# Six small edits in a two-layer conditioned mixture-of-experts kernel: warming products, first bias, lane tables, one row turn, shares

## What is computed

```
x = x + _L0_ffn_ref(_L0_cond_ref(x, cond_8, weight, mask, bias), router_w, expert_weights)
x = x + _L1_ffn_ref(_L1_cond_ref(x, cond_8, W_base, b_base, As, Bs), gate_w, exp_gate, exp_up, exp_down, sh_gate, sh_up, sh_down)
```

```
topk_vals, topk_idx = top_k(softmax(x @ router_w.T), 2)
topk_w = topk_vals / (topk_vals.sum(-1) + 1e-06)
out = ((combined + remap_bias) * weights).sum(axis=0)      # remap_bias = probs of the two
```

## Time and profile before

| | |
|---|---|
| runs, median of 3 | 354.28 us (354.05 to 354.62) |
| the profiled execution, its own time | 354.84 us |
| its span, first to last instruction | 353.1 us |
| granted TensorE clock, mean | 1.000 |
| busy: PE, PE weight load | 346.8 us (98%), 216.9 us (61%) |
| busy: DVE, ACT, POOL | 239.1 us (68%), 172.5 us (49%), 147.8 us (42%) |
| DMA | 47.42 MB, 134 GB/s over the span |

### The profile page before, as it was taken

How to read it: one execution, slowest core, us unless ns; L and a number is a source line. 1 busy time by engine, 2 the same in 40 slices (tenths; PEclk the granted TensorE clock), 3 DMA queues, 4 the chain that set the end, 5 groups by cost and what they waited for, 6 DMA issues and landing times.

```text
span 353.1 us, 8015 instructions
## 1 busy us (share of the span) xinstructions
PE 346.8 (98%) x2746; PEld 216.9 (61%) x2747; DVE 239.1 (68%) x618; ACT 172.5 (49%) x296; POOL 147.8 (42%) x252
## 2 busy tenths in 40 slices
PE   8999999999999999999999999999999999999996
PEld 4444444454455454566458777777777777766655
DVE  1369899997766754789985555555555565655696
ACT  1178468558558648544541333333333333424493
POOL 4049475656646644000012355555555555422000
PEclk9999999999999999999999999999999999999999
DMA  7976122442343321010005334444454353111963
GB/s 275 407 305 218 59 100 81 159 159 91 129 156 85 136 80 61 0 61 0 2 1 187 113 132 162 174 146 156 138 177 163 132 156 119 61 46 49 351 226 119
DMA packets 20505, 47.42 MB, mean 134 GB/s; under 512 B 2432, under 2 KB 11392, under 8 KB 20480
## 3 DMA queue, kind: packets, MB, share of 16 engines
q1 hardware_dynamic: 17024, 37.65, 29.9%
q0 software_dynamic: 3456, 9.44, 8.4%
HBM read 29.25 MB, written 8.91 MB: 108 GB/s over the span
## 4 chain that ended last, share of the span: by engine, by line
PE 81%; DVE 13%; ACT 3%; issue 3%; DVEq 0%; ACTq 0%
PE bank L1156 58%; PE bank L1167 7%; PE bank L1330 4%; PE bank L1433 4%; PE bank L1408 2%; DVE x L863 2%; PE bank L1182 2%; DVE prod L1045 2%; DVE yg L959 1%; ACT w1s L658 1%; ACT sil L669 1%; DVE acts L1053 1%; PE bank L1172 1%; PE bank L1246 1%; PE bank L1257 1%
## 5 line engine op out<-in xcount | busy, mean ns | idle before, releaser
L1156 PE MATMUL bank<-w0s,hs 128*128 128x512 f16 x384 | 86.5, 379 | 0.9 <-DVE x L863 0.9
L513 POOL TENSOR_TENSOR w1s<-piece,w1s 128x170 f16<-128x170 f32 x128 | 60.9, 514 | 42.4 <-ACT piece L600 42.4
L522 POOL DMA_INDIRECT rows<-token_store,row_in x36 | 35.0, 971 | 77.7 <-DVE row_in L990 45.3
L863 DVE SCALAR_TENSOR_TENSOR x<-bank,coef,x 128x256 f32<-128x256 f32 x128 | 54.4, 476 | 14.2 <-PE bank L1156 14.1
L1156 PEld LDWEIGHTS bank<-w0s,hs 128*128 128x128 f16 x384 | 37.1, 98 | 42.9 <-DVE x L863 1.4
L1156 PE MATMUL bank<-hs,w1s 128*128 128x512 f16 x264 | 59.4, 379 | 0.3 <-DVE prod L1045 0.2
L1156 PE MATMUL bank<-w1s,rT 128*128 x336 | 54.5, 313 | 0.0
L528 POOL DMA_INDIRECT results<-yb,row_out x36 | 35.7, 992 | 35.9 <-ACT yb L707 35.9
L701 ACT ACTIVATE ract<-prod 128x352 f16<-128x352 f32 x36 | 17.9, 497 | 53.9 <-DVE prod L1128 44.0
L1156 PEld LDWEIGHTS bank<-hs,w1s 128*128 128x128 f16 x264 | 25.3, 98 | 29.2 <-DVE prod L1045 1.3
L1156 PEld LDWEIGHTS bank<-w1s,rT 128*128 128x128 f16 x336 | 31.7, 98 | 14.7 <-issue 0.2
(11 more groups left out here) (183 smaller groups left out, 498.4 us busy)
## 6 DMA issues: line engine op xcount, KB each, us to landing
piece<-w SPq DMA_DIRECT2D x16, 680.0 KB, 4.0
xrow<-w1s SPq DMA_DIRECT2D x8, 704.0 KB, 3.6
xrow<-w1s SPq DMA_DIRECT2D x8, 384.0 KB, 3.0
w1s<-results SPq DMA_DIRECT2D x6, 512.0 KB, 10.0
x<-wc SPq DMA_DIRECT2D x4, 512.0 KB, 5.0
w1s<-xT SPq DMA_DIRECT2D x4, 512.0 KB, 9.7
w1s<-w SPq DMA_DIRECT2D x4, 512.0 KB, 9.1
x<-x SPq DMA_DIRECT2D x4, 512.0 KB, 8.4
```

The costliest lines, as they stand in the source:

```text
L513: ins = nc.gpsimd.tensor_tensor(w1s[:, LO, at], piece[:, i % 2, part], w1s[:, HI, at], ALU.subtract)
L522: pool.indirect_dma_start(rows[:, i % 2], None, token_store, bass.IndirectOffsetOnAxis(row_in[:, slot_tile(i):slot_tile(i) + 1], 0)).then_ ...
L863: nc.vector.scalar_tensor_tensor(x1[:, t], bank[(n + a) % 4][:, h * D:(h + 1) * D], coef[:, t, e:e + 1], x1[:, t], ALU.mult, ALU.add).then ...
L1156: mm = nc.tensor.matmul(out_ap, l, r, start=(i == 0), stop=(i == len(terms) - 1))
```

## The change

Six edits:

1. `FILL` goes from 14 to 4.
2. In `shares0` the sum over `ex` is issued first and isn't linked, and the scaling of `REC` is merged into the instruction that makes `coef`. The four instructions of the bias become `bias0`, called after m = 0, j = 1 for part 0, and directly after `shares0` for the other parts.
3. ACT's `exps(0)` comes after `w0_scaled(1)`.
4. The last 12 of 32 lane instructions go to POOL, behind its last piece and a new semaphore `s_slots` that `slots(1)` sets; `inverse()` waits for them by `s_lanes`. DVE issues 20, in `accumulate(0)`. The entries of `between` for i = 8, 9 and 10 move up by one.
5. The rows of tile 2 are turned in step -1 (before tile 1's gate product) and not in step 0.
6. `shares1` is called in `accumulate(1)`, one part after each of its four adds, and the written-out steps at the end of DVE's loop become three.

```diff
@@ -77,7 +77,7 @@
     WARM = 8
-    FILL = 14
+    FILL = 4
     DIRECT = (0, 2)
@@ -264,6 +264,8 @@
             "s_hot",
+            "s_slots",
+            "s_lanes",
             "s_inv",
@@ -366,7 +368,7 @@
 
-        def run_tiles(eng, step, ahead, beside=None):
+        def run_tiles(eng, step, ahead):
 
@@ -376,8 +378,6 @@
                 step(s, s % 2)
-                if beside is not None:
-                    beside(s)
 
@@ -513,6 +513,12 @@
 
+            pool.wait_ge(sm["s_pclo"], NP)
+            pool.wait_ge(sm["s_slots"], 1)
+            for n in range(5 * ENTRIES // 8, ENTRIES):
+                ins = nc.gpsimd.tensor_scalar(hot_lo[:, n], lane16[:], slot_lo[:, n:n + 1], None, ALU.is_equal)
+            ins.then_inc(sm["s_lanes"], 1)
+
             pool.wait_ge(sm["s_tok"], 16 * B)
@@ -569,8 +575,8 @@
             w0_hi(1)
+            w0_scaled(1)
             exps(0, PARTS[0], 1.0 / (SH0 * SW))
-            w0_scaled(1)
             h_hi(0, 2)
@@ -791,14 +797,17 @@
                 dve.wait_ge(sm["s_exp"], part + 1)
+                nc.vector.tensor_reduce(SUM[:, tiles], ex[:, tiles], AX.X, ALU.add)
                 link(nc.vector.tensor_tensor(t1[:, tiles], ex[:, tiles], t1[:, tiles], ALU.mult))
                 link(nc.vector.tensor_reduce(S2[:, tiles], t1[:, tiles], AX.X, ALU.add))
-                link(nc.vector.tensor_reduce(SUM[:, tiles], ex[:, tiles], AX.X, ALU.add))
                 link(nc.vector.scalar_tensor_tensor(S2[:, tiles], SUM[:, tiles], EPS_TOPK, S2[:, tiles], ALU.mult,
...
                 link(nc.vector.reciprocal(REC[:, tiles], S2[:, tiles]))
-                link(nc.vector.tensor_scalar(REC[:, tiles], REC[:, tiles], 1.0 / (SH0 * SW), None, ALU.mult))
-                link(nc.vector.tensor_tensor(coef[:, tiles], t1[:, tiles], each(REC, tiles), ALU.mult))
+                link(nc.vector.scalar_tensor_tensor(coef[:, tiles], t1[:, tiles], 1.0 / (SH0 * SW), each(REC, tiles),
+                                                    ALU.mult, ALU.mult))
+
+            def bias0(tiles):
+
                 link(nc.vector.tensor_tensor(t1[:, tiles], t1[:, tiles], coef[:, tiles], ALU.mult))
@@ -865,6 +874,8 @@
                         h_lo(0, 3)
+                    if m == 0 and j == 1:
+                        bias0(PARTS[0])
                     if m == 0 and j == 2:
@@ -873,6 +884,7 @@
                         shares0((m + 1) // 2, PARTS[(m + 1) // 2])
+                        bias0(PARTS[(m + 1) // 2])
                     if j == 0 and m >= 3 and m % 2 == 1:
@@ -890,21 +902,21 @@
 
-            def shares1(s):
-
-                if s == TILES - 5:
+            def shares1(q):
+
+                if q == 0:
                     dve.wait_ge(sm["s_exp"], 4)
...
                     link(nc.vector.tensor_reduce(S2, t1[:], AX.X, ALU.add))
-                if s == TILES - 4:
+                if q == 1:
                     link(nc.vector.reciprocal(REC, S2))
...
                     link(nc.vector.tensor_tensor(coef[:], t1[:], each(REC, ALL), ALU.mult))
-                if s == TILES - 3:
+                if q == 2:
                     link(nc.vector.tensor_tensor(t1[:], oh1[:], coef[:], ALU.mult))
                     link(nc.vector.tensor_reduce(W1, t1[:], AX.X, ALU.add))
-                if s == TILES - 2:
+                if q == 3:
                     link(nc.vector.tensor_tensor(t1[:], oh2[:], coef[:], ALU.mult))
@@ -949,8 +961,10 @@
                     link(nc.vector.tensor_copy(slot_hi[:], idx[:].rearrange("p k t -> p (k t)")))
-                    link(nc.vector.scalar_tensor_tensor(slot_lo[:], slot_hi[:], -float(P),
-                                                        st[:, 7:9].rearrange("p k t -> p (k t)"), ALU.mult, ALU.add))
+                    nc.vector.scalar_tensor_tensor(slot_lo[:], slot_hi[:], -float(P),
+                                                   st[:, 7:9].rearrange("p k t -> p (k t)"), ALU.mult,
+                                                   ALU.add).then_inc(sm["s_slots"], 1)
+                    dve.wait_ge(sm["s_slots"], 1)
 
@@ -1066,15 +1080,18 @@
                     t = c * TPB + q
-                    if c == 0:
+                    if c == 0 and q < 2:
                         hot_lanes(2 * q)
-                        if q < TPB - 1:
-                            hot_lanes(2 * q + 1)
+                        hot_lanes(2 * q + 1)
+                    if c == 0 and q == 2:
+                        hot_lanes(2 * q)
                     if c == 1 and q == TPB - 2:
...
                                                    ALU.mult, ALU.add).then_inc(sm["s_acc"], 1)
+                    if c == 1:
+                        shares1(q)
                     if c == 2 and q == 1:
@@ -1086,8 +1103,8 @@
 
-            between = {2: lambda: take_logits(1, 0, ALL), 3: chosen, 5: groups, 6: lambda: slots(0), 7: lambda: hot_tiles(0, 0), 8: lambda: hot_lanes(7),
-                       9: lambda: hot_tiles(0, 1), 10: lambda: hot_tiles(1), 11: lambda: hot_tiles(2, 0),
+            between = {2: lambda: take_logits(1, 0, ALL), 3: chosen, 5: groups, 6: lambda: slots(0), 7: lambda: hot_tiles(0, 0),
+                       8: lambda: hot_tiles(0, 1), 9: lambda: hot_tiles(1), 11: lambda: hot_tiles(2, 0),
                        12: lambda: hot_tiles(2, 1), 13: lambda: tile_experts(0), 14: lambda: tile_experts(1),
@@ -1133,7 +1150,7 @@
             dve.wait_ge(sm["s_ahi"], EARLY)
-            run_tiles(dve, step, 4, shares1)
+            run_tiles(dve, step, 2)
             step(TILES, TILES % 2)
@@ -1366,6 +1383,7 @@
                 pe.wait_ge(sm["s_hot"], 2)
+                pe.wait_ge(sm["s_lanes"], 1)
                 pe.wait_ge(sm["s_acc"], TPB)
@@ -1397,16 +1415,22 @@
 
+            def turn_rows(i, par):
+
+                pe.wait_ge(s_row[par], landed(i, par))
+                for a in range(2):
+                    for k in range(KT):
+                        o = (a * KT + k) * P
+                        mm = nc.tensor.transpose(bank16[4][:, o:o + P], rows[:, par, o:o + P], ident16[:])
+                mm.then_inc(sm["s_ra"], 1)
+
             def step(s, par, down_at, gate_at, down_own=None, gate_own=None):
...
                 i = s + 2
-                if known(i) and again(i):
-                    pe.wait_ge(s_row[par], landed(i, par))
-                    for a in range(2):
-                        for k in range(KT):
-                            o = (a * KT + k) * P
-                            mm = nc.tensor.transpose(bank16[4][:, o:o + P], rows[:, par, o:o + P], ident16[:])
-                    mm.then_inc(sm["s_ra"], 1)
+                if known(i) and again(i) and not (isinstance(s, int) and s == 0):
+                    turn_rows(i, par)
+                if isinstance(s, int) and s == -1:
+                    turn_rows(2, 0)
                 i = s - 1
```

## The result

The changed kernel takes 352.64 us (median of 6 runs, 352.03 to 352.91), the kernel before 354.45 us on the same chip (6 runs, 353.88 to 355.4). The ratio is 0.9945 with a 95% interval of 0.9929 to 0.9961: faster by 1.8 us, and by more than 0.2%. The prediction said 352.6. The profiled execution takes 352.29 us with a span of 350.5, against 354.84 and 353.1, so the two traces lie 2.6 us apart where the medians lie 1.8 apart. Where the other 0.8 us come from is the first thing that the experiments have to tell.

What follows compares the result with a forecast made beforehand. The chain of waits lay on PE for 81% of the span and DVE for 13%; -0.5 -0.2 -0.35 -0.3 +0.25 -0.6 = -1.7 us gave 352.6 against the median of 354.28, range 351.2 to 354.4.

Steps and rivals of the forecast that it cites:

- The end of 1.07: Start: upper end of the gain from ten fewer warming products, 1.07 us if the clock rises by 5.2 us.
- The rival of a late rise: Masked weights' stage from 5.20 on: each us at 1.2 GHz costs 0.5, kernel slower, up to 358.7; chance 0.07.
- the 11.1 from which the rival would have decided: Masked weights' stage: kernel slower by over 0.7 us if PE's clock isn't up before 11.1 us.
- In part 2 PE leads: nothing: Layer 0, part 2 of `shares0`: PE leads there, so the shorter routing gains nothing.
- from there to 141 us PE doesn't wait: Layer 0: after its wait for DVE at 55.47, PE has no wait until 141 us.
- The price: Lane tables: one lane on POOL costs 0.28 to 0.43 us, so twelve take 3.4 to 5.2 us.
- the sign of a wrong price: Lane tables: lane instructions on DVE further apart than 0.17 us, with PE waiting for `prod`, would show the forecast wrong.
- The locked lanes: Lane tables: DVE's lanes wait for POOL's whole instructions, +2.1 us against the sum, 354.7 (half: 353.6); chance 0.16.
- their issue hangs on the same PE stage, so the distance stays: First routed tiles: tile 2's rows land 4.2 us after issue, PE waits 0.7 us; 0.25 us lost.
- all of it: Start and tile 2's turn: clock rises early and the rows are there, -0.6 -0.65 us, 351.4; chance 0.14.
- The early gain doesn't carry: Start and layer 0: loads, ACT or POOL set the pace by 37 us, or bias delays DVE: 353.3; chance 0.13.

Runs made afterwards that it cites:

- t3: Changed kernel with the old `shares0`, its bias and the place of `exps` put back: 353.8 us, ratio 0.997 to the kernel before.
- r3: Changed kernel with the first two tiles' rows turned one product group sooner, so tile 2's rows are fetched sooner: 353.15 us, ratio 0.9939 to the kernel before.
- t1: Changed kernel with the 384 KB load of the first `own_dn` held back until tile 2's rows are turned: 352.08 us, ratio 0.9928 to the kernel before.
- p4: Changed kernel with WARM = 0 and FILL = 0, no warming product at all: 353.84 us, ratio 0.9969 to the kernel before.
- t2: Changed kernel with the first `own_dn` load held back until tile 2's rows are turned, and FILL = 0: 351.45 us, ratio 0.991 to the kernel before.
- p1: Kernel before with FILL = 4 in place of 14 alone: 354.44 us, ratio 0.9983 to the kernel before.

## Why the prediction was right, and where its steps were off

The total is right to 0.1 us, 352.6 against 352.64, and the medians' difference of 1.81 is near the sum of the terms as read from two traces: 0.54 + 0.20 + 0.50 + 0.32 - 0.37 + 0.59 = 1.78. Two sizes were off in opposite ways and hid each other. That the total is right to 0.1 us is luck: layer 0 varies by 0.37 us and the turn by 0.23 from one execution to the next.

**Ten warming products fewer (0.5 forecast; 0.54).** The size is right, the way to it was not. I took the rise at 6.2 us for a fixed date and halved what lay before it. The rise has no such date: 4.0 to 6.9 us in executions of like starts. But since PE has no gap from 1.25 on, ten products removed are worth their columns at full pace, 0.54, whenever it comes; the forecast's 0.57 came out near that because its rise lay inside the stage. The end of 1.07 was no bound of the edit at all. The rival of a late rise is refuted for this change (no later with four small products than with fourteen), and shown real for another: without any warming the rise came at 9.9 us, close to the 11.1 from which the rival would have decided. One reading beside it was rough: the float32 products of 512 columns follow every 0.43 us and not 0.45, which changes no term.

**Shorter `shares0`, bias between the sums (0.2 and 0.35 forecast; 0.70 together in the traces, 0.9 at equal lengths of `las`).** The wait at the third logits is gone, 0.20 us at that place, and t3 brings it back. That it arrives at the end too was assumed: DVE carries it on, but in the two first traces a longer `las` eats it. The bias cost nothing in its gap, as costed: 33.80 to 34.61, with DVE still waiting behind it. The second size was too small, 0.48 for 0.35 at the wait of 55.47, and 0.21 more for a wait that the sum had put at nothing. "In part 2 PE leads: nothing", and "from there to 141 us PE doesn't wait", were wrong: PE waited for `lbw` at 81.15, and that wait goes too. I had read the waits of PE's products only; this one is shown in the row of the weight load. With `las` the distance is 66.84 to 67.21 for the same code, so over the runs the whole part is worth 0.6 to 1.0 us where 0.55 was forecast.

**Lanes to POOL (0.3 forecast; 0.32).** The gain is capped by the wait that it takes away, and the cap held. The price was low: 0.65 us for a lane on POOL, not 0.28 to 0.43, so twelve take 8.1 us in place of 3.4 to 5.2 and end at 166.5 instead of 165.5. It made no difference, since nothing wants them before 175.9. DVE's loss beside POOL was costed at 1.1 us in all, 0.06 for each lane that meets it; it is 0.7 us, up to 0.05 a lane (1.79 against 1.39 for eight). The lanes are 0.22 apart where 0.17 was to be the sign of a wrong price, but `prod` came in time. The locked lanes are refuted: a DVE lane doesn't wait for POOL's whole 0.65 us. The Trainium skill (SBUF — State Buffer, Who interferes with whom) says that a DVE instruction in a two-port mode, into which `tensor_scalar` can go, and GpSimd shut each other out for a whole instruction. Here 20 `tensor_scalar` of 128x128 float16 with a scalar per partition ran beside POOL's unbroken row of them with a median of 297 ns and none above 385, where they took 241 to 250 in the kernel before. No view shows in which mode they ran, so what is measured is only that this form, in whatever mode, isn't shut out for a whole instruction.

**Row turn one step sooner (-0.25 forecast; -0.37).** The mechanism is as costed: PE waits for the gather with tile 1's other twelve products behind the wait. It arrives 4.2 us after its issue in the kernel after as it had before, and the loss was undersized by 0.1 us: the shown wait is 0.53, about 0.7 with the modelled end as forecast, and the distance grew by 0.24 to 0.47 over the runs that wait. But the step "their issue hangs on the same PE stage, so the distance stays" gave the wrong cause. r3 issues the gather 2.1 us sooner and gains nothing; t1 leaves its issue alone, holds one load back, and gains 0.65. The gather is late because a DMA engine that it shares with the load ahead of it is held up by an instruction packet, and the load's packets in it come first. The rival "all of it" rested on the median gather; its turn term (0.35 us sooner than before) came true in p4 by itself and in t1 and t2 by the edit.

**`shares1` out of the loop (0.6 forecast; 0.59).** Right in both halves: the steps came out at 3.35, 3.33 and 3.11, and the ten instructions are free in `accumulate(1)`.

**The early gain doesn't carry** is refuted for the start, whose gain arrives whole: the distances behind it are no longer than before but for the turn's, by its own edit. For the 0.20 us of the first bias it came half true, since `las` took them in the first pair of traces.

**What stays open.** Nothing moved the instruction packet on purpose, and what sets its moment isn't shown; eleven traces against p4 tie it to the late load by their times alone. The view of the DMA doesn't name single engines, so that the late packets are one engine's is read from their following one another. t1's ratio overlaps the changed kernel's. t2's, 1.1 to 1.2 us below the changed kernel's two, lies below both intervals, but some 0.2 of it belongs to the four small products. A smaller load wasn't tried. What sets the moment of the clock's rise from execution to execution isn't shown by any run.

## What to carry to other kernels

Before two traces are compared, take out what belongs to the execution: here the moment at which PE's clock rises moved a span by up to 1.5 us, more than any single part of the change, while most distances between two of PE's products repeat to some hundredths. Where one doesn't, look for the instruction that differs: here the 0.37 us of scatter in layer 0 were one DVE instruction beside POOL. Where PE waits for a gather, ask what is in the same queues before asking when it is issued: on PE's distances, holding back a load that isn't wanted yet gained 0.65 us and issuing the gather 2.1 us sooner nothing. And look for PE's waits in the rows of the weight loads too, since a wait for stationary data stands there.

## What the hardware showed that was not expected

- In five executions with unbroken products from 1.25 us on, PE's clock went from the lower to the higher level at 4.0, 4.7, 5.1, 6.2 and 6.9 us; with products only from 4.83 on, at about 9.9. The kernel before, which does the same each time, ran from 353.78 to 356.06 us beside p1 to p4; half of 3 us of spread in the rise would be 1.5 of these 2.3 us, if those runs spread as the traces do.
- Float32 products of 256 columns in four column groups take a step of 0.43 us at the lower level and 0.215 at the higher.
- A `tensor_scalar` with a scalar per partition takes POOL 0.65 us on 128x128 float16 (0.60 to 1.07), more than twice its select of the same shape.
- One 16 KB packet of the instruction queue took 0.92 us. The last eleven packets of a 384 KB load began when it ended and were through 1.8 us behind the others (189.87 to 191.65), and the last of a small gather came behind them: it landed 4.2 us after its issue in one run and 6.1 in another. Without that load ahead it landed within 3.4 us.
- DVE's `las`, with both inputs in SBUF and POOL beside it, took 0.41 to 0.77 us in eleven executions of the same instruction.
